# Both ends of a second block rewritten: unit 0's second chunk tapped in a bank of its own, the layer norm's root first; own buffers for the last units and their energies in chunks

## What is computed

```python
pooled = x.mean((2, 3))
hdn = _ln(pooled @ w_fc1.T, ln1_w, ln1_b)
dyn_w = (hdn @ w_fc2.T).reshape(b * c, 1, 5, 5)
out = depthwise_conv(x, dyn_w)                  # 5 by 5, one kernel per image and channel
out = ln2_w * (out - mean_c) * rsqrt(var_c + EPS) + ln2_b
out = gelu(einsum('bchw,oc->bohw', out, w_expand))
gx = sqrt(sum(out ** 2, axis=(2, 3)))
nx = gx / (gx.mean(1) + EPS)
out = gamma * (out * nx) + beta + out
return einsum('bohw,co->bchw', out, w_shrink) + x
```

## Time and profile before

| | us |
|---|---|
| median of 3 runs | 850.76 (849.52 to 851.38) |
| the profiled execution | 850.89 |
| its span, first to last instruction | 849.2 |
| first block, to | about 502 |
| block two, from there to the end | about 347 |
| PE, DVE, POOL, ACT busy | 782.8, 616.4, 468.0, 408.8 |

### The profile page before, as it was taken

One profiled execution on the slowest core, in us unless ns is written; L12 is line 12 of the kernel. 1 busy time (PEld: TensorE's weight loads), 2 busy tenths in 40 slices (PEclk: granted clock), 3 DMA queues, 4 the chain that ended last, 5 costly groups with the idle time before them and its releaser, 6 DMA issues. The chain is left out here.

```text
span 849.2 us, 15642 instructions
## 1 busy us (share of the span) xinstructions
PE 782.8 (92%) x5399; PEld 637.7 (75%) x5399; DVE 616.4 (73%) x1130; ACT 408.8 (48%) x497; POOL 468.0 (55%) x458
## 2 busy tenths in 40 slices
PE   5999999999999999999999968587899999999796
PEld 5999998999999999999999966354444545444231
DVE  4666666666666666658888866988799898998944
ACT  5591003777771000000000014369899999999771
POOL 2333333333333333337888854788889889897510
PEclk9999999999999999999999987889899999999899
DMA  6760000000000000000000010132233443334314
GB/s 146 154 173 0 0 0 2 0 0 0 0 1 1 0 0 0 0 1 2 0 0 0 0 49 0 47 77 58 52 79 81 112 97 94 78 80 91 83 32 100
DMA packets 61572, 35.81 MB, mean 42 GB/s; under 512 B 41504, under 2 KB 59488, under 8 KB 61536
## 3 DMA queue, kind: packets, MB, share of 16 engines
q1 hardware_dynamic: 61536, 35.36, 18.0%
HBM read 17.85 MB, written 9.37 MB: 32 GB/s over the span
## 5 line engine op out<-in xcount | busy, mean ns | idle before, releaser
L481 PE MATMUL psum<-line_hi,taps_hi 128*128 128x256 f32 x1270 | 202.5, 291 | 11.8 <-DVE taps_lo L377 8.5
L495 PE MATMUL psum<-line_lo,taps_hi 128*128 128x256 f32 x1270 | 202.2, 291 | 0.8 <-DVE line_lo L430 0.8
L489 PE MATMUL psum<-line_hi,taps_lo 128*128 128x256 f32 x1270 | 202.0, 291 | 0.0
L430 DVE SCALAR_TENSOR_TENSOR line_lo<-psum,rest 128x256 fp32r<-128x256 f32 x254 | 108.2, 426 | 123.4 <-POOL rest L262 114.9
L481 PEld LDWEIGHTS psum<-line_hi,taps_hi 128*128 128x128 f32 x1270 | 176.6, 192 | 12.9 <-issue 9.3
L495 PEld LDWEIGHTS psum<-line_lo,taps_hi 128*128 128x128 f32 x1270 | 176.3, 191 | 1.9 <-DVE line_lo L430 1.7
L489 PEld LDWEIGHTS psum<-line_hi,taps_lo 128*128 128x128 f32 x1270 | 176.7, 191 | 0.0
L262 POOL TENSOR_TENSOR rest<-x,line_hi 128x256 f32<-128x256 f32 x127 | 82.8, 652 | 167.8 <-DVE line_hi L421 167.8
L759 POOL TENSOR_TENSOR part<-part,prod 128x960 f32<-128x960 f32 (+2 forms) x64 | 145.2, 2269 | 25.0 <-ACT prod L826 17.8
L262 POOL TENSOR_TENSOR rest<-by_h,line_hi 128x256 f32<-128x256 f32 x127 | 91.5, 720 | 83.4 <-DVE line_hi L421 83.4
L314 ACT ACTIVATE by_h<-x (+1 forms) x128 | 85.7, 669 | 105.0 <-DVE x L410 103.3
(11 more groups left out here) (138 smaller groups left out, 749.5 us busy)
## 6 DMA issues: line engine op xcount, KB each, us to landing
stage<-in_x_dram SPq DMA_DIRECT2D x32, 256.0 KB, 4.1
rstd_wide<-rstd_dram SPq DMA_DIRECT2D x30, 256.0 KB, 5.4
out_dram<-x SPq DMA_DIRECT2D x28, 256.0 KB, 5.5
crossed<-x SPq DMA_DIRECT2D x16, 256.0 KB, 3.6
crossed<-x SPq DMA_DIRECT2D x16, 240.0 KB, 3.5
out_dram<-x SPq DMA_DIRECT2D x8, 128.0 KB, 2.5
rstd_dram<-rstd SPq DMA_DIRECT2D x15, 64.0 KB, 1.5
fc_in<-in_L_conv_w_fc_dram SPq DMA_DIRECT2D x2, 100.0 KB
```

What stands on the lines that cost most here:

```text
L430: dve.scalar_tensor_tensor(out=line_lo[:, (slot + 1) % SLOTS, :, part], in0=as_lines(line_ps[slot][:, 0:LINE]), scalar=0.0, in1=as_lines(r ...
L481: mm = pe.matmul(line_ps[slot][:, 0:LINE], taps_hi[:, s, d, :], line_hi[:, slot, :, d:d + WP], start=(d == 0), stop=(d == OFFSETS - 1))
L489: pe.matmul(line_ps[slot][:, 0:LINE], taps_lo[:, s, d, :], line_hi[:, slot, :, d:d + WP], start=False, stop=False, skip_group_check=True)
L495: mm = pe.matmul(line_ps[slot][:, 0:LINE], taps_hi[:, s, d, :], line_lo[:, slot, :, d:d + WP], start=False, stop=(d == OFFSETS - 1), skip_ ...
```

## The change

At the start, POOL waits for each product of ACT by itself and not for all five. ACT calls a Sqrt on an unused cell first and takes the layer norm's root ahead of the two copies to `x_hi`. DVE's `split_low(0)` goes behind `own_ready`, PE's weight folding behind the fc2 product. `second_chunk` taps chunk 1 of unit 0 first, starting from zero in bank 6 (`out_ps`), without waiting for a convolution; the ordinary steps then tap chunk 0, and `add_first_part` sums three terms for chunk 1 and two for chunk 0.

At the end, unit 14's `normed` is laid over `crossed`, unit 15's over `squares`, unit 15's grown values over `prod`, the last shrink weights over `var` and `spread` over `part`; the waits on the shared ones go. From unit 13 on, expansions alternate between two pairs of banks (`FREE_CONV`). ACT's squares of unit 13's second half go to DVE; the last half's squares are summed in two chunks with an energy column each. ACT calls a Sqrt on an unused cell behind the squares of unit 15. PE's `respond(B - 2)` also waits for unit 15's variance. PE puts unit 15's expansions ahead of three of the four shrinks of units 12 and 13, and the last `respond` ahead of the fourth. DVE puts `finish` of chunk 1 of unit 12 and both of unit 13 behind the last `respond`.

```diff
-        FREE_CONV = 4 * (LAST - 1)
+        FREE_CONV = 4 * (LAST - 2)
...
-        spread = prod[:, 0, :, :].rearrange("p j w -> p (j w)").rearrange("p (g k c) -> p g k c", k=SUBS, c=P)
...
+        spread = part[:, 0, :, :].rearrange("p j w -> p (j w)").rearrange("p (g k c) -> p g k c", k=SUBS, c=P)
+        last_wide = prod[:, :, :, :].rearrange("p (m h) j w -> p m h (j w)", m=HALVES)
...
-        energy = sb("energy", [P, HALVES, 2])
+        energy = sb("energy", [P, HALVES, 3])
...
-            return psum[:, (6, 7, 6, 7, 4, 5, 0, 1)[k - 2 * (LAST - 3)], :]
+            return psum[:, (6, 7, 2, 6, 4, 5, 0, 1)[k - 2 * (LAST - 3)], :]
...
+        def grown(u):
+            return wide[:, :, :, u % WIDE, :] if u < LAST else last_wide
+        last_shrink = var[:, :].rearrange("p (m c) -> p m c", m=HALVES)
+        late_normed = crossed[:, 0, :, :].rearrange("p j w -> p (j w)")
+        def normed_of(u):
+            return normed[:, :] if u < LAST - 1 else late_normed if u == LAST - 1 else squares[:, :]
...
             def add_product(u, n):
...
-                pool.wait_ge(prod_ready, N_ACT * (u + 1))
+                pool.wait_ge(prod_ready, N_ACT * u + n + 1)
...
             def norm(u):
...
-                if u > 0:
+                if 0 < u < LAST - 1:
...
-                pool.tensor_tensor(normed[:, :], image, rstd_wide[:, :], ALU.mult).then_inc(normed_ready, 1)
+                pool.tensor_tensor(normed_of(u), image, rstd_wide[:, :], ALU.mult).then_inc(normed_ready, 1)
...
             def make_spread():
...
-                pool.wait_ge(part_step, PART_STEPS * UNITS)
+                pool.wait_ge(tap_step, N_DVE * LAST)
...
             def gelu(u, m, c):
...
-                if m == 0 and u >= WIDE:
+                if m == 0 and WIDE <= u < LAST:
...
-                act.activation(wide[:, m, :, u % WIDE, c * COLS:(c + 1) * COLS], exp_set(4 * u + 2 * m + c),
+                act.activation(grown(u)[:, m, :, c * COLS:(c + 1) * COLS], exp_set(4 * u + 2 * m + c),
...
             def add_squares(u, m):
...
-                               wide[:, m, :, u % WIDE, :], ACT.Square,
+                               grown(u)[:, m, :, :], ACT.Square,
...
+            act.activation(mean_sq[:, 0:1], kept["ident"][:, 0:1], ACT.Sqrt)
+            act.wait_ge(pads, 1)
+            act.wait_ge(hid_var, 1)
+            act.activation(hid_stat[:, 2:3], hid_stat[:, 1:2], ACT.Sqrt, bias=eps_col[0:B, :],
+                           scale=1.0 / CR).then_inc(hid_sd, 1)
...
-            act.wait_ge(pads, 1)
...
-            act.wait_ge(hid_var, 1)
-            act.activation(hid_stat[:, 2:3], hid_stat[:, 1:2], ACT.Sqrt, bias=eps_col[0:B, :],
-                           scale=1.0 / CR).then_inc(hid_sd, 1)
...
-            add_squares(LAST - 2, 1)
...
+            act.activation(hid_stat[:, 0:1], eps_col[0:B, :], ACT.Sqrt)
...
+            root_energy(B - 2)
...
-            root_energy(B - 2)
...
             def take_tap(u, i):
...
-                    return add_part(u)
+                    return add_part(u) if u > 0 else add_first_part()
...
-                    dve.wait_ge(conv_done, 2 * (u + 1))
+                    dve.wait_ge(conv_done, 1 if u == 0 else 2 * (u + 1))
...
-                    src, rows = src[:, CROWS - rows.start:rows.stop - rows.start, :], slice(CROWS, rows.stop)
+                    src, rows = src[:, 0:CROWS - rows.start, :], slice(rows.start, CROWS)
...
-            def first_chunk():
-                dve.wait_ge(conv_done, 1)
+            def second_chunk():
...
-                for i in range(N_DVE - 1):
+                src, rows, cols, weight = place(0, *DVE_TAPS[-1])
+                first_acc = out_ps.rearrange("p (j w) -> p j w", w=W)
+                link(dve.tensor_scalar(first_acc[:, 0:rows.stop - CROWS, cols], src[:, CROWS - rows.start:rows.stop - rows.start, :],
+                                       weight, None, ALU.mult))
+                for i in range(N_DVE - 2):
...
-                    here = acc[:, 0, rows.start:CROWS, cols]
-                    link(dve.scalar_tensor_tensor(out=here, in0=src[:, 0:CROWS - rows.start, :], scalar=weight, in1=here, op0=ALU.mult, op1=ALU.add))
+                    here = first_acc[:, 0:rows.stop - CROWS, cols]
+                    ins = dve.scalar_tensor_tensor(out=here, in0=src[:, CROWS - rows.start:rows.stop - rows.start, :],
+                                                   scalar=weight, in1=here, op0=ALU.mult, op1=ALU.add)
+                    link(ins)
+            def add_first_part():
+                dve.wait_ge(part_step, PART_STEPS)
+                dve.wait_ge(conv_done, 2)
+                dve.wait_ge(tap_step, N_DVE - 1)
+                second = inner[:, 0, CROWS:ROWS, :]
+                link(dve.scalar_tensor_tensor(out=second, in0=part[:, 0, CROWS:ROWS, :], scalar=1.0,
+                                              in1=out_ps.rearrange("p (j w) -> p j w", w=W), op0=ALU.mult, op1=ALU.add))
+                link(dve.scalar_tensor_tensor(out=second, in0=second, scalar=1.0, in1=acc[:, 0, CROWS:ROWS, :],
+                                              op0=ALU.mult, op1=ALU.add))
+                dve.scalar_tensor_tensor(out=inner[:, 0, 0:CROWS, :], in0=part[:, 0, 0:CROWS, :], scalar=1.0,
+                                         in1=acc[:, 0, 0:CROWS, :], op0=ALU.mult, op1=ALU.add).then_inc(tap_step, 1)
...
             def norm(c):
...
-                dve.wait_ge(exp_done, 4 * LAST)
-                dve.tensor_tensor(normed[:, c * COLS:(c + 1) * COLS],
+                dve.tensor_tensor(squares[:, c * COLS:(c + 1) * COLS],
...
             def add_squares(u, m):
...
-                dve.wait_ge(energy_summed, B - 1)
-                grown = wide[:, m, :, u % WIDE, :]
-                dve.tensor_tensor_reduce(dump[:, :].rearrange("p (a n) -> p a n", a=2), grown, grown, 1.0, 0.0,
+                dve.wait_ge(energy_summed, u // 2)
+                image = grown(u)[:, m, :, :]
+                dve.tensor_tensor_reduce(dump[:, :].rearrange("p (a n) -> p a n", a=2), image, image, 1.0, 0.0,
...
+            def add_squares_chunk(c):
+                dve.wait_ge(gelu_done, 4 * LAST + 3 + c)
+                dve.wait_ge(energy_ready, 2 * LAST + 1 + c)
+                image = grown(LAST)[:, 1, :, c * COLS:(c + 1) * COLS]
+                dve.tensor_tensor_reduce(dump[:, 0:2 * COLS].rearrange("p (a n) -> p a n", a=2), image, image, 1.0, 0.0,
+                                         ALU.mult, ALU.add, energy[:, 1, 1 + c:2 + c]).then_inc(energy_ready, 1)
             def sum_energy(b):
-                dve.wait_ge(energy_ready, 4 * (b + 1))
+                dve.wait_ge(energy_ready, 4 * (b + 1) + (b == B - 1))
...
             def respond(b):
...
-                dve.tensor_tensor(shrink_now[:, :, :], kept["shrink_t"][:, :, :],
+                dve.tensor_tensor(shrink_now[:, :, :] if b < B - 1 else last_shrink, kept["shrink_t"][:, :, :],
...
+            dve.memset(energy[:, :, 2:3], 0.0)
...
-            split_low(0)
...
+            split_low(0)
...
-            first_chunk()
+            second_chunk()
...
+            add_squares(LAST - 2, 1)
...
+            add_squares(LAST - 1, 1)
...
-            add_squares(LAST - 1, 1)
-            finish(LAST - 3, 1)
...
-            finish(LAST - 2, 0)
-            add_squares(LAST, 1)
+            add_squares_chunk(0)
+            add_squares_chunk(1)
...
-            finish(LAST - 2, 1)
-            for u in (LAST - 1, LAST):
+            finish(LAST - 3, 1)
+            for u in (LAST - 2, LAST - 1, LAST):
...
-            for m in range(HALVES):
-                pe.matmul(exp_ps[:, 0, m * P:(m + 1) * P], kept["centre"][:, :, :].rearrange("p o c -> p (o c)"),
+            def fold_weights():
...
+            fold_weights()
...
-                    mm = pe.matmul(exp_set(e)[:, hp, :], expand_w[half, m, :], normed[half, c * COLS:(c + 1) * COLS],
+                    mm = pe.matmul(exp_set(e)[:, hp, :], expand_w[half, m, :], normed_of(u)[half, c * COLS:(c + 1) * COLS],
...
             def respond(b):
...
+                if b == B - 2:
+                    pe.wait_ge(var_step, VAR_STEPS * UNITS)
...
-                    pe.wait_ge(finished, k - 1)
+                    pe.wait_ge(finished, min(k - 1, 2 * (LAST - 3) + 1))
...
-                        mm = pe.matmul(out_bank(k)[C * hp:C * hp + C, :], shrink_now[:, m, :],
-                                       wide[:, m, hp, u % WIDE, c * COLS:(c + 1) * COLS],
+                        mm = pe.matmul(out_bank(k)[C * hp:C * hp + C, :], (shrink_now if b < B - 1 else last_shrink)[:, m, :],
+                                       grown(u)[:, m, hp, c * COLS:(c + 1) * COLS],
...
+            expand(LAST - 1, 1, 1)
...
-            expand(LAST - 1, 1, 1)
+            expand(LAST, 0, 0)
+            expand(LAST, 0, 1)
+            expand(LAST, 1, 0)
+            expand(LAST, 1, 1)
...
-            for m in range(HALVES):
-                for c in range(2):
```

(24 more changed lines are left out.)

## The result

The changed kernel takes 838.38 us (median of 4, 836.51 to 839.35), against 851.07 for the kernel before on the same chip: a ratio of 0.985, 95% interval 0.982 to 0.988. The forecast was 838.4, so its sum came out to a tenth of a microsecond. Its terms did not: the start gave 1.8 us more than forecast and the tail 1.4 less. The span of the profiled execution is 837.0 us, 12.2 shorter.

The account below looks back on a forecast made before the run. The middle was held to be in balance, leaving idle time in start and tail. Start 3.2 + 4.9 - 1.1 = 7.0 us, tail 6.2 - 0.5 - 0.3 = 5.4, together 12.4: forecast 838.4 us, range 834.5 to 842.8.

Parts of the forecast that it names:

- The middle is only shifted: Middle of block two: all engines in balance, so the repeating pattern moves as a whole and the change takes no work out.
- The root 3.6 us earlier, `tap_all` 3.2: Start: table loaded early brings the layer norm's root 3.6 us forward; DVE's own queue then sets `tap_all`, gain 3.2.
- 4.9 us for DVE's wait, less 1.1 for `add_first_part`: Start, unit 0: chunk 1 first removes DVE's 4.89 us wait for the first convolution; three smaller sums lose 1.1.
- POOL is no bound: Start: POOL's four adds end at 523.6, its x_hi, x_lo and dyn for unit 2 at 529.2, before `inner(0)` at 529.6.
- The clock, 1.5 us, kept as a bound and not taken: Start, unit 2's convolution: with 2.3 us of idle time, not 6.1, PE's clock may stay up, giving 1.5 us more.
- Unit 15's square 3.3 us earlier: Tail: alternating banks and squares moved to DVE free ACT, which squares at 806.75 instead of 810.02, gain 3.3 us.
- The added squares end the wait for the variance at 810.0, 3.3 behind `inner`: Tail: DVE has a `finish` (0.75) and added squares (2.28 plus 0.08) before unit 15's variance, until 810.0.
- PE at half clock, 0 to 1.6, of which I took 0.3: Tail: PE idles 2.9 us before unit 15's statistics and may do them and two expansions at half clock; 0.3 us loss.
- Five shrinks of 1.87, ended 31.7 behind `inner`: Tail: PE, free at about 829.0, does five last shrinks in 9.35 us, ended at 838.4; gain 6.2 us.
- The stores, 0.5: Tail's end: 2.1 MB at 222 GB/s take 9.4 us, to 841.7; 0.5 us added for the crowd.
- the clock helps: Rival, 12%: unit 2's convolution and the last shrinks run at clock 1.00; gains 8.5 and 7.0, total 835.3 us.
- the tail moves to the stores: Rival, 8%: DVE's squares run into each other or stores move under 180 GB/s; tail gives 3.0, total 840.8 us.

Follow-up runs that it names:

- e1: The start's edits alone on the kernel before, with the old tail: median 843.16 us (ratio 0.991), start stretch 295.80, tail 42.33.
- e2: The tail's edits alone on the kernel before, old start, without POOL's new wait: median 847.35 us (0.996), start stretch 305.60, tail 38.27.
- e3: The changed kernel with DVE's old order for unit 0 (chunk 0 first, one sum for both chunks): start stretch 302.12 us, 6.4 more.
- e4: The changed kernel with POOL's old wait for all five products of a unit: start stretch 299.26 us, 3.5 more.
- e6: The changed kernel with 12 extra products on PE in its idle time ahead of unit 15's statistics: tail 37.02 us, 1.5 shorter.
- e7: The changed kernel with finish of unit 12's chunk 1 moved ahead of DVE's last respond: tail 36.70 us, 1.8 shorter; median 837.08 (0.983).
- e10: The changed kernel with extra PE products in the start and ahead of unit 15's statistics, and unit 12's finish moved ahead of DVE's last respond: median 833.27 us (0.979).
- e8: The changed kernel with POOL's norm of unit 14 held until DVE's squares of unit 13 are done: squares 2.28 us, tail 43.22.

## Why the prediction was right, point by point

- *The middle is only shifted.* Right; e1 and e2 show the ends to be independent.
- *The root 3.6 us earlier, `tap_all` 3.2.* Measured 3.5 and 3.5; the two `split_low` just fit. The drain that the Trainium skill adds to a table load (ScalarE: Activation LUTs, section What ACT_TABLE_LOAD costs), weighed there, would have made it 1.2 less. The rows show none.
- *4.9 us for DVE's wait, less 1.1 for `add_first_part`.* The wait fell by 4.7 and the three steps took 2.1 us, 0.9 more than the one. e3 gives the pair as 4.4, its wait having come back at 5.50. `inner(0)` 7.3 us earlier, for 7.0.
- *POOL is no bound.* It was none, but by 0.4 us: its weights for unit 2 ended at 529.57, `inner(0)` at 529.95. I priced POOL's new wait at nothing in the middle and used it silently in the start; e4 shows that it is worth 3.5 us.
- *The clock, 1.5 us, kept as a bound and not taken.* This is the step of the start that was mis-sized. PE idled some 2 us, not 6, ahead of unit 2's convolution, DVE's two waits for variances shrank by 1.0 and 0.5 us, and the start gave 8.8 us. Two changes behind them were in no working, and they cancel: the step from unit 3 to 4 took 23.40 us in place of 21.98, the two from 4 to 6 together 35.99 in place of 37.35. I took it for the less likely case by the short gaps elsewhere.
- *Unit 15's square 3.3 us earlier.* Right: 0.04 us behind `inner`, in place of 3.31.
- *The added squares end the wait for the variance at 810.0, 3.3 behind `inner`.* Measured 4.6. The price of 2.28 came from a row with POOL idle; beside `norm` it was 3.88.
- *PE at half clock, 0 to 1.6, of which I took 0.3.* Measured by e6: 1.5, a miss of 1.2. With the one before it put unit 15's first gelu at 14.97 behind `inner`, where my working had 14.1.
- *Five shrinks of 1.87, ended 31.7 behind `inner`.* Ended at 32.3. They took 8.8 us, not 9.35, and started 1.2 late.
- *The stores, 0.5.* The last store came 1.6 later behind the last `finish` than before, and e7 got back 1.8, so this is a miss of 1.1 to 1.3. I worked with 222 GB/s, the best microsecond of the old trace; over the 11 us from 825 the queues moved 191 on average (150 to 219 in a microsecond). And I left out SP's issues: 12 in a row, of which four took about twice as long as before. The last store was issued 2.3 us behind its `finish`, and landed no later behind its issue than before.
- So the tail gave 4.0, not 5.4, and the start 8.8, not 7.0; together 0.3 more than forecast, and the first block took 0.5 of it back. That the total met the forecast is in part luck. None of the rivals happened whole, but two did in part, *the clock helps* at the start and *the tail moves to the stores* at the end.

What stays open: why a loss in units 0 to 2 grows by up to 2 us until unit 6 (e3), beyond the one place that e10 shows. A lower clock between units 3 and 4 goes with it in e3's trace, but no run tried it. Open too is what paced the last stores, SP's issues or the queues.

## What to carry to other kernels

When an edit takes the first bound of a start away, look up what each other engine has ready at that time: here one line on POOL decided over 3.5 of 8.8 us, with 0.4 us to spare. Price an instruction that is moved from a row with the same neighbour running beside it, and a row of transfers both by what the queues carry over its whole length and by the time that each issue takes. Where PE idles ahead of work that others wait for, and the trace has it at half clock behind the gap, useless products in the gap can pay: 52 of them and one moved `finish` brought 838.4 to 833.3.

## What was not expected of the hardware

- DVE's multiply and sum of 128 by 2048 values from SBUF took 3.65 to 4.04 us beside a POOL product of two SBUF operands (2.35 us), and 2.28 without it. POOL lost nothing. DVE's taps of 496 to 504 columns, with one operand in PSUM, took 0.74 to 0.75 us before POOL had started its adds and beside them (e8, and the nine profiles named there; for the taps the changed kernel's start).
- After 3.5 us without work PE ran at a clock of 0.59 on average for the next 4 us; with products in the gap, at full clock (1.00, e6).
- Two runs of the same start differ by 0.64 us in unit 1 (the changed kernel and e6), and two of the old start by 0.6 in unit 0 (e2 and the kernel before), by when the clock rises.
- Twelve stores of 256 and 128 KB issued one behind the other from SP took 0.60 to 0.67 us an issue in eight cases and 1.13 to 1.41 in four, 10.5 us in all.
